# A transformer block with self and cross attention on one core: the order of all engines' stages laid out anew, and VectorE's list of waits made fuller

## What is computed

```python
c_proj = jax.nn.silu(c) @ W_mod + b_mod
shift_a, scale_a, gate_a, shift_m, scale_m, gate_m = jnp.split(c_proj, 6, axis=-1)
x_norm = modulate(_ln(x), shift_a, scale_a)
qkv = x_norm @ W_qkv + b_qkv
...
attn_w = jax.nn.softmax(jnp.einsum('bhqd,bhkd->bhqk', q, k) * scale, axis=-1)
...
x = x + gate_a[:, None] * attn_out
q_c = _ln(x) @ W_qc + b_qc
kv_c = _ln(context) @ W_kvc + b_kvc
...
x = x + c_attn_out
x_norm2 = modulate(_ln(x), shift_m, scale_m)
h = jax.nn.gelu(x_norm2 @ W_mlp1 + b_mlp1)
h = h @ W_mlp2 + b_mlp2
x = x + gate_m[:, None] * h
```

## Time and profile before

| what | us |
|---|---|
| median of 3 runs | 827.2 (826.37 to 833.03) |
| the profiled execution, its own time | 829.95 |
| its span | 828.0 |
| TensorE busy | 797.6 (96%) |
| VectorE busy | 630.0 (76%) |
| ScalarE busy | 484.2 (58%) |
| GpSimd busy | 391.8 (47%) |

### The profile page before, as it was taken

The page is one execution under the profiler, slowest core; times in us unless marked ns, Lnnn a source line. Parts: engine busy times, 40 slices in busy tenths (PEclk is TensorE's granted clock), DMA queues, the critical chain, the costliest instruction groups (busy, mean ns, idle before and its releaser), DMA issues.

```text
span 828.0 us, 18919 instructions
## 1 busy us (share of the span) xinstructions
PE 797.6 (96%) x6968; PEld 613.2 (74%) x6968; DVE 630.0 (76%) x1368; ACT 484.2 (58%) x921; POOL 391.8 (47%) x451
## 2 busy tenths in 40 slices
PE   5899899999999999999999999999999999999897
PEld 3667567778787878778787877778787877777576
DVE  5758998887878788887878788887878787873631
ACT  2162657567575857567575847567475757666242
POOL 3455345464455545464454546465455544441310
PEclk9788999999999999999999999999999999999799
DMA  7435454443444253343444353453444342211101
GB/s 261 157 126 153 136 174 127 121 137 91 129 123 135 78 155 116 113 145 91 128 123 136 79 149 121 112 140 97 128 115 144 79 140 93 67 51 52 28 1 39
DMA packets 92900, 95.03 MB, mean 115 GB/s; under 512 B 17993, under 2 KB 79562, under 8 KB 92426
## 3 DMA queue, kind: packets, MB, share of 16 engines
q1 hardware_dynamic: 91946, 92.77, 37.8%
q10 hardware_dynamic: 864, 1.07, 0.4%
HBM read 38.55 MB, written 4.32 MB: 52 GB/s over the span
## 4 chain that ended last, share of the span: by engine, by line
PE 89%; DVE 6%; DMA 2%; issue 1%; SPq 1%; ACT 1%; POOL 0%; DVEq 0%; ACTq 0%; POOLq 0%
PE bank L833 24%; PE scan L935 15%; PE pv L880 14%; PE bank L867 13%; PE score L945 7%; PE bank L858 7%; PE bank L847 5%; PE bank L807 2%; DVE MX_y L1294 2%; DVE MX_x L1294 1%; DMA OT<-in_bv 1%; DVE PN L1213 1%; DMA out_x<-y 0%; DVE PT L1204 0%; PE pv L792 0%
## 5 line engine op out<-in xcount | busy, mean ns | idle before, releaser
L1095 ACT ACTIVATE P<-score 128x512 f32<-128x512 f32 x512 | 282.2, 597 | 187.5 <-PE score L945 186.7
L1294 DVE TENSOR_REDUCE MX_x<-scan 128x2 fp32r<-128x512 f32 x256 | 166.6, 677 | 39.0 <-PE scan L935 38.8
L1294 DVE TENSOR_REDUCE MX_y<-scan 128x2 fp32r<-128x512 f32 x256 | 165.8, 683 | 25.6 <-PE scan L935 23.2
L833 PE MATMUL bank<-xT_y,W 128*128 128x256 f32 x960 | 131.6, 290 | 2.5 <-DVE xT_y L1159 2.5
L833 PEld LDWEIGHTS bank<-xT_y,W 128*128 128x128 f32 x960 | 121.1, 194 | 8.2 <-issue 3.5
L867 PE MATMUL bank<-w_down,HH 128*128 128x256 f32 x512 | 124.4, 388 | 0.0
L935 PEld LDWEIGHTS scan<-KS_y,QS_y 63*128 63x128 f32 x512 | 70.7, 189 | 53.1 <-DVE MX_y L1294 30.4
L935 PE MATMUL scan<-KS_y,QS_y 63*128 63x256 f32 x512 | 103.1, 315 | 5.2 <-DVE MX_y L1294 4.5
L867 PEld LDWEIGHTS bank<-w_down,HH 128*128 128x128 f32 x512 | 92.7, 189 | 19.9 <-issue 5.8
L935 PE MATMUL scan<-KS_x,QS_x 63*128 63x256 f32 x512 | 101.2, 316 | 3.9 <-DVE MX_x L1294 2.8
L945 PE MATMUL score<-QS_x,KS_x 64*128 64x256 f32 x512 | 100.8, 314 | 0.4 <-ACT P L1095 0.4
(11 more groups left out here) (139 smaller groups left out, 1241.1 us busy)
## 6 DMA issues: line engine op xcount, KB each, us to landing
KS_x<-SK SPq DMA_DIRECT2D x96, 128.0 KB, 3.0
KS_y<-SK SPq DMA_DIRECT2D x96, 128.0 KB, 2.5
...
x_in<-in_x SPq DMA_DIRECT2D x16, 256.0 KB, 3.1
tn_c<-in_ctxT SPq DMA_DIRECT2D x16, 256.0 KB, 2.7
c_in<-in_ctx SPq DMA_DIRECT2D x16, 256.0 KB, 3.0
gate_a<-d_gate SPq DMA_DIRECT2D x16, 256.0 KB, 3.9
```

What stands on the lines that cost most here:

```text
L833: last = nc.tensor.matmul(to[:, i * N:(i + 1) * N], w[p][:, c, (blk + i) * 128:(blk + i + 1) * 128], xT[k][:, q, c, :], start=(n == 0), st ...
L1095: nc.scalar.activation(P[:, s % 8, :, :].rearrange("p a n -> p (a n)"), score_bank[s % 2][:, :], ACT.Exp, scale=SCALE).then_inc(s_exp, 1)
L1294: nc.vector.tensor_reduce(MX[s1][:, half, col:col + NB], scan_bank[n % NSCAN][:, :].rearrange("p (a n) -> p a n", a=NB), AXIS.X, ALU.max, ...
```

## The change

All five tables are written anew, for the steady steps ("A", "B") and for the special ones at both ends. The stages, their number and the instructions in them are the same; they stand elsewhere. Of the tables two rows are shown, then all of the rest of the change: VectorE waits for more.

```diff
 PE_PLAN = {
...
-    "A0": [("mod_m", 0, 10), ("q_xb", 1, 12), ("q_xa", 1, 13)],
...
+    "A-1": [],
+    "A0": [("mod_m", 0, 0), ("q_xb", 1, 4), ("k_xa", 1, 6), ("q_xa", 1, 10)],
...
@@ -1122,6 +1120,8 @@
                 if k in "xc":
                     wait(dve, s_mean[k], b)
                     wait(dve, s_ve[k], b)
+                else:
+                    wait(dve, s_xn[k], b)
                 for a in range(NB):
                     last = nc.vector.bn_stats(stats[k][:, a, :], src[:, a, :])
                 last.then_inc(s_stats[k], 1)
@@ -1168,7 +1168,7 @@
             def split_copied(name, k, b):
-                src = bank[USE[name, b] % NBANK]
+                src = full(dve, name, b)
                 dve.wait_ge(s_hi[name], b + 1)
...
@@ -1201,6 +1201,7 @@
             def turned(s, half, b):
                 m = half_index(s, b, half)
                 dve.wait_ge(s_pv, 2 * m + 2)
+                wait(dve, s_pn, m)
...
@@ -1217,9 +1218,9 @@
-                if half == 0 and s == "x" and b >= 2:
+                if s == "x" and b >= 2:
                     dve.wait_ge(s_full, FILLS["out_y", b - 2] + 1)
-                if half == 0 and s == "y" and b + 1 < B:
+                if s == "y" and b + 1 < B:
                     dve.wait_ge(s_full, FILLS["out_x", b + 1] + 1)
...
@@ -1227,11 +1228,13 @@
             def maxima(s, half, b):
                 dve.wait_ge(s_scan_done, SCANS[s, b] + PAIRS * (half + 1))
+                wait(dve, s_row[s][half], 4 * 16 * b)
...
             def out_x(b):
                 dve.wait_ge(s_x_bias, b + 1)
                 wait(dve, s_x1_bias, b)
+                wait(dve, s_xn["y"], b)
...
             def out_y(b):
                 dve.wait_ge(s_x1_bias, b + 1)
                 wait(dve, s_x2_bias, b)
+                wait(dve, s_xn["m"], b)
```

More of the change, by code:

```diff
@@ L28 @@
 SP_PLAN = {
[L29 to L41, removed]
@@ L42 @@
-    "B": [],
[L43 to L47, removed]
@@ L48 @@
-    "BB+0": [("q_y1", -1, 0), ("out", -4, 0), ("max_y0", -1, 4)],
-    "BB+1": [("gate_m", -2, 0)],
-    "BB-1": [],
+    "A": [("gate_a", 0, 0), ("c_in", 1, 0), ("k_x", 1, 2), ("st_c", 0, 3), ("x_in", 2, 3), ("max_x0", 0, 4),
+          ("q_y0", -1, 5), ("mr_c", 0, 5), ("q_y1", -1, 6), ("max_x1", 0, 6), ("q_x", 1, 8), ("st_x", 2, 9),
+          ("xT_in", 2, 10), ("max_y0", -1, 10), ("cT_in", 1, 13), ("gate_m", -2, 14), ("mr_x", 2, 14),
+          ("k_y", 0, 14), ("max_y1", -1, 14), ("out", -3, 14)],
@@ L148 @@
 }
 POOL_PLAN = {
-    "A": [],
-    "A1": [],
+    "A": [("gate", -1, 12)],
+    "A1": [("T_x", 1, 8), ("x_bias", 0, 12), ("norm_c", 0, 15)],
     "AB+0": [],
-    "AB-1": [("gate", -1, 14)],
-    "B": [("gate", -1, 0), ("x1_bias", -2, 1), ("norm_x", 1, 5), ("T_x", 1, 5), ("root_c", 0, 5), ("root_y", -1, 5),
-          ("x_bias", 0, 6), ("norm_c", 0, 6), ("x2_bias", -3, 9), ("T_c", 0, 10), ("sum0", -3, 10),
-          ("norm_m", -2, 12), ("root_x", 2, 13), ("sum1", -3, 13), ("T_m", -2, 13)],
-    "B-1": [("root_c", 1, 0), ("norm_x", 1, 9), ("root_x", 2, 12), ("x_bias", 1, 15)],
@@ new lines @@
+    "B": [("norm_x", 1, 0), ("x1_bias", -2, 0), ("T_x", 1, 2), ("root_y", -1, 2), ("root_c", 0, 2),
+          ("x2_bias", -3, 3), ("x_bias", 0, 4), ("norm_c", 0, 4), ("sum0", -3, 8), ("T_c", 0, 8), ("root_x", 2, 9),
+          ("norm_m", -2, 9), ("T_m", -2, 11), ("sum1", -3, 15)],
+    "B-1": [("norm_x", 1, 0), ("root_x", 2, 0), ("root_c", 1, 8), ("x_bias", 1, 10)],
+    "B0": [("clear1", 0, 0), ("clear2", 0, 1), ("gate", 0, 1), ("T_x", 0, 1), ("clear0", 0, 2), ("root_x", 2, 2),
+          ("norm_c", 0, 2), ("clear_V", 0, 6), ("clear3", 0, 6), ("T_c", 0, 6), ("norm_x", 1, 6), ("root_c", 1, 6),
+          ("norm_x", 2, 6), ("root_y", 0, 6), ("clear4", 0, 13)],
@@ L169 @@
+    "B1": [("T_x", 0, 0), ("T_c", 0, 2), ("root_x", 2, 5)],
[5 rows of a table added]
+    "BB-1": [("root_y", -1, 1), ("root_c", 0, 1), ("norm_c", 0, 1), ("T_c", 0, 3), ("norm_m", -2, 3),
+          ("x_bias", 0, 11), ("sum0", -3, 14)],
 }
```

125 lines of the change are left out of this document (69 added, 56 removed), and 80 rows, old and new, of tables (DVE_PLAN, PE_PLAN, POOL_PLAN).

## The result

The changed kernel is slower by about 0.9%: a median of 838.8 us against 829.8, ratio 1.0094 with a 95% interval of 1.0060 to 1.0128. Two further sets of executions gave 1.0089 (1.0056 to 1.0122) and 1.0089 (1.0055 to 1.0123). The prediction was 823.9, with a range to 832.5, so the time lies outside it, and on the other side of the kernel before. The 829.8 is the median of six executions; the prediction started from 827.2, the median of the first three.

What follows compares the result with a forecast made beforehand. TensorE was taken as the bound, fully busy in the 46.50 us steady periods and idle only at the ends. Start -5.5, middle +2.8 and end -0.6 gave -3.3 us, from 827.2 to 823.9; range 816.5 to 832.5.

Steps and rivals of the forecast that it cites:

- The head ahead of the first scan: Start: bias product no longer waits for its transfer, -1.75 us; first reduction's gate operations wait less, -0.25 us.
- mod_m, w2 and w3: Start: mod_m at full clock after the first scan, half counted, -0.9 us; weights w2, w3 moved into VectorE's waiting time, -1.2.
- Twelve projections fewer ahead of B1: Start, between A1's last slot and B1's first: 12 projection matmuls instead of 24, -1.4 us.
- The start as a whole: All sections before the steady periods: gains together -5.5 us, bounds -3 to -8.
- The steady period: Twelve middle periods: extra changes between kinds of matmul on TensorE cost +0.27 us each, +3.2 in all.
- The stall: Middle: PN on VectorE, lengthened to 1.62 us during a GpSimd addition, no longer is; 0.4 us taken back, middle +2.8.
- The new waits: VectorE's added waits are met microseconds earlier, so nothing counted; one late by 1 us each period would cost +12.
- The margins of SyncE and GpSimd: Steady period: inputs T_c, x's transposed input and norm_m ready 0.8, 0.7 and 0.3 us before needed.
- rival (a): Steady periods: GpSimd's and SyncE's chain becomes the bound, inputs reach TensorE late, +13 us, 836.9 us; chance 0.13.
- The end: Last sections: A15 -0.4, B15 -0.1, A16 +1.7, B16 -1.3 and -0.5 after them; together -0.6 us.
- The tail's -0.5: After the last sections: a piece of down put ahead of up, where TensorE idled 6.4 us; -0.5, between 0 and -1.7.
- (c): Rival: start's gain doesn't carry, since A1 and A2 wait for SyncE and transfers; start -1.8, total 827.6 us; chance 0.2.

## Why the prediction was wrong, by its own steps

- **The base.** The sum was taken from 827.2, the median of three executions; six give 829.8. That is 2.6 us of the 14.9 between forecast and measurement, and has nothing to do with the change.
- **The head ahead of the first scan, -1.75 and -0.25.** Right: the bias product waits no more, the gate product starts at 12.1 us (12.4 forecast) and the first scan came 3.2 us earlier in the first pair of profiles, 2.2 in the mean of all.
- **mod_m, w2 and w3, -0.9 and -1.2.** mod_m took 1.96 us instead of 3.59, as expected. What w2 and w3 gave was not measured by itself.
- **Twelve projections fewer ahead of B1, -1.4.** Wrong. They were counted as gone from the end of A1 and not as arrived in B1, where they stand now (x125 instead of x113). The run with new A1 and B1 alone measured +0.7 us (+-0.9), or +1.0 (+-0.5) at equal clock.
- **The start as a whole, -5.5.** It failed: its measured share is -0.1 us the first time and +0.6 the second (+-0.7 each). This is the step that made the prediction wrong. It asked only where the clock could get better (mod_m), and left the old stretches' clocks otherwise as they were. For the dense projections that the change takes out from between the scores of B0 it had no term at all, that is nothing, and did not ask what is then left on TensorE: B0 took 19.1 to 20.4 us, 13.8 and more of them at half clock, where the 15.2 us at 0.87 had been read. At equal clock the new start is worth 2.8 to 3.6 us, half to two thirds of the 5.5; what is missing there is about the size of the mistake on the twelve projections (2.4). A mean clock lower by 0.006 takes 3.5 us back. B0 is shown for half of that clock, and the rest is open.
- **The steady period, +0.27.** Right: 46.80, and 561.8 against 559.2 us over twelve, +2.6, with +2.8 forecast. The number of passages between kinds of matmul, priced by rows, was a good measure. The stall was right too: PN takes 0.46 us in the mean of 64 instead of 0.63, TensorE is busy for all of the twelve periods, and since it was so before but for 0.4 us, hardly any time follows. What was missed is that "A" and "B" also serve A2 and B2 (25.35 and 14.34 us instead of 24.58 and 14.02 in the first profiles, +1.1; +1.7 in the means above). The margins of SyncE and GpSimd held, so rival (a) did not happen.
- **The new waits, 0.** Not contradicted, and not settled: 2.6 us (+-1.4) in the plain means, 1.0 (+-0.5) at equal clock.
- **The end, -0.6.** Wrong: +1.5 by the profiles' sections, +2.1 by the means, and more than 1 us was one of the prediction's own signs of being wrong. In the first profile A15 and B15 were as forecast (-0.6 together). A16 was mis-sized, +2.8 instead of +1.7: the count of matmuls gave +1.7, and T_y's wait of 0.93, a stage put earlier than its input, was not looked for. B16 gave -1.1 of the -1.3. The tail's -0.5 is not to be seen: 48.6, 49.2 and 50.9 us in the changed kernel's three profiles, 49.4 before.
- **The rivals.** (c) had the outcome of the start right, "doesn't carry", and its sign, A1 at 57 us or later, came (58.8). Its reason was not: TensorE goes into A1 without a wait for a transfer in the changed kernel's profile. It was given 0.2 and 827.6 us; with A2, B2 (+1.1) and an end of +2.1 instead of -0.6 it would have given 831.4 us.
- **The range.** It was built on one profiled execution. A start whose sections move by up to 9 us from one execution to another, with nothing changed but waits, needed a wider range on both sides, and a sum of terms of 0.25 us for it was finer than what it was read from.
